# 2304 places for a sender block in place of 2560: a fifth slot tile of 64 lanes

## The chip, the cores and the metric

The kernel runs on one core of one Trainium2 chip. What counts is the device time of one launch, in microseconds (us). The core has TensorE (PE in the profile, with its weight loads as PEld), VectorE (DVE), ScalarE (ACT), GpSimd (POOL) and SyncE (SP, which here only issues DMAs).

## The reference

Four graph networks run one after the other on the same graph of 3125 nodes with 128 features and 53125 directed edges; each adds to `x`, and a layer norm follows. Cut to what matters:

```python
# L0: gated network, 2 rounds; edge_type has 8 values
trans = einsum('nh,tdh->tnd', h, edge_W[l]);  msgs = trans[edge_type, src]
agg = segment_sum(msgs, dst);                 h = relu(gru(agg, h))
# L1: three relational layers
msg = xw[etype, src] / count(etype, dst);     agg = segment_sum(msg, dst)
h = res + relu(agg + x @ root + bias)
# L2: normed sum over receivers, gathered at the sender
msgs = norm * x[col];                         agg = segment_sum(msgs, row)
# L3: means of edge_attr over dst and over src, and a two-layer network
```

The edges are sorted by `dst`; `src` is in no order. All is float32.

## The kernel before

A **sender block** is 126 nodes; there are `TB = 25`. Each edge has a place in its sender's block, in the order of the edges. A block has `CAP` places, and four places side by side are one lane's record: a row of 4 x 128 numbers in the DRAM tensor `chunks`. 128 such rows, so 512 places, are a **slot tile**; `QS = 5` tiles a block make 2560 places, and `NQ = 125` tiles in all. The fullest block of this input has 2226 edges. Tiles are numbered by turn first: tile `n` is turn `n // 25` of block `n % 25`, so tiles 100 to 124 are the fifth turn of the 25 blocks.

The program has these stages, which follow one another in the trace.

- **First loop** (about 100 to 604 us): 52 groups of 1024 edges. GpSimd gathers message rows (L694), PE sums them by receiver (L834), counts marks (L842, whose result is 56 lanes high) and puts each edge's payload into its place (L848). VectorE then unpacks the places (`slots`).
- **First layer's tiles** (676 to 834 us): for each of 125 tiles VectorE makes a one-hot (L1901), PE spreads the block's rows over the lanes in four products (`spread_slots`, L956), ScalarE copies the result from PSUM to `xs` (L1301, 6 buffers), and SP stores it to `chunks` (L561).
- **First layer's sums** (837 to 1070 us): for each of 149 windows of 21 receivers GpSimd gathers 128 rows of `chunks` (L694), VectorE makes one-hots, and PE sums in four products (`sum_window`, L984). Every 12 windows follows a `transform` (L969).
- **Layers 2 to 4** (1172 to 2238 us): tiles and window sums are interleaved by a written order (`plan`, `joined`). In a layer's tail, two tiles stand for three windows. In layers 3 and 4 GpSimd also scatters attributes (L703) between its gathers.
- **Targets** (2290 to 2490 us): rows are spread and scattered to `chunks` (L1174, L792).
- **Block sums** (2494 to 2637 us): for each block, its five slot tiles are loaded back (L679, with the attributes, L680) and summed in 4 products of 144 columns each (L1198); after the next block's third tile the block is turned by two small products (L1186 and L1187; L1187's result is 16 lanes high).

A float32 product is in the trace as two records, each with its own weight load. A record of 128 x 128 is called a pair below. In the built programs each matmul carries the part of the array that it uses: it is the whole one (128 rows by 128 columns) for nearly all, 128 rows by 64 columns for L842, 128 by 32 for L1187 and 32 by 128 for L1147.

If a block had more edges than places, flags would send the program to a slow general path (`general`); this input does not take it before or after.

Of the kernel before, what the change touches and what calls it, by code (L numbers as in the profile page):

```python
# [16 lines left out]
ALU = mybir.AluOpType  # L17
ACT = mybir.ActivationFunctionType
# [3 lines left out]
P = 128  # L22
# [4 lines left out]
TB = 25  # L27
NV = TB * P
BS = 126
# [6 lines left out]
A = 16  # L36
# [12 lines left out]
SPAN = 512  # L49
QS = 5  # L50
NQ = TB * QS
# [1 line left out]
QCOLS = 4 * TB  # L53
NEAR = 3 * QCOLS
NEAR_STEPS = (24, 40)
CAP = QS * SPAN
WD = 21
WT = WD * T
NW = -(-NODES // WD)
# [6 lines left out]
NGRP = -(-NW // GW)  # L66
RECORD_COLS = 4 * P + 4
FAR_CODE = 32767
RECS = NQ * P
RS, DS, SS, XS, NS = 6, 4, 4, 6, 3  # L70
RANKS = TB * CAP
YW = 5
# [74 lines left out]
def graph_kernel(nc, xT_d, dst_rows_d, dst_d, src_d, typ_d, mark_d, w_d, b_d, iota_d, out_d):  # L147
    with ExitStack() as ctx:
# [291 lines left out]
        def plan(k):  # L440
# [9 lines left out]
                at.append((NQ + v if k == 1 else when, 1, "sums", v))  # L450
            return [(kind, n) for _, _, kind, n in sorted(at)]

        def tile_no(k, i):

            return JOINED[i] if k >= 3 else i
# [60 lines left out]
        def _(eng):  # L516
# [32 lines left out]
            def layer(k):  # L549
                if k == 2:  # L550
                    eng.wait_ge(q("lanes_ready"), 2)
                    eng.dma_start(targets_d.rearrange("(a r) p -> r a p", a=5), trow_u8[0:NWP * 4 // 5])\
                       .then_inc(q("lanes_stored"), 16)
                def store_tile(k, i):
                    n = tile_no(k, i)
                    after(eng, "x1_evac", k, i + 1)
                    if k == 1:
                        eng.wait_ge(q("code_put"), i + 1)
                    cols = RECORD_COLS if k == 1 else 4 * P
                    at = (n % TB * QS + n // TB) * P  # L560
                    eng.dma_start(x1_d[at:at + P, 0:cols], xs[:, i % XS, 0:cols])\  # L561
                       .then_inc(q(f"x1_stored_{i % XS}"), 16)
                    ahead = n // QS + NS - 1
                    if k >= 3 and n in (20, 25, 30):
                        for s in {20: (), 25: (6,), 30: (7, 8)}[n]:
                            lanes_load(k, s)
                    elif n % QS == 0 and ahead < TB:
                        lanes_load(k, ahead)
                    if k == 2 and i in (10, 18):
                        inv_load((i - 10) // 8)  # L570
                    if k >= 3 and n in (27, 36):
                        after(eng, "agg_evac", k - 1, NTRI)
                        inv_load((n - 27) // 9)
                    if k == 3 and n == 42:
                        attrs_sent(eng, 2)
                        attr_load(attrs_1, AT[3])
                    if k == 3 and n == 60:
                        attr_load(attrs_0, AT[5])
                    if k == 4 and n == 42:
                        attrs_sent(eng, 3)  # L580
                        attr_load(attrs_1, AT[4])
                    if 2 <= k < 4 and n == NQ - 1:
                        for s in range(NS - 1):
                            lanes_load(k + 1, s)

                if k == 1:
                    for i in range(NQ):
                        store_tile(1, i)
                    eng.wait_ge(q("inv_ready"), INV_PIECES)
                    eng.dma_start(inv_d, acc[TYPE_ROWS, 0:NU]).then_inc(q("inv_stored"), 16)  # L590
                    after(eng, "acc_evac", 1, NGRP)
                    general(1)
                    attrs_sent(eng, 1)
                    attr_load(attrs_0, AT[2][:6])
                    eng.wait_ge(q("attr_loaded"), 48)
                    after(eng, "gru_h", 1, NCH)
                    attr_load(attrs_1, AT[2][6:])
                    for s in range(NS - 1):
                        lanes_load(2, s)
                    return  # L600
                for kind, j, i in joined():
                    if kind == "tile":
                        store_tile(j, i)
                    if kind == "sums" and i >= GW and i % GW == 5 and i // GW + 1 < NGRP:
                        after(eng, "agg_evac", j, 4 * (i // GW))
                        inv_load(i // GW + 1)
                after(eng, "acc_evac", 4, NGRP)
                for j in (2, 3, 4):
                    general(j)
# [66 lines left out]
            for i in range(NQ):  # L676
                if i >= GR:
                    eng.wait_ge(q("gcn_sum"), i - GR + 1)
                eng.dma_start(grec[:, i % GR, 0:4 * P], x1_d[i * P:(i + 1) * P, 0:4 * P]).then_inc(q(f"x1_stored_{i % GR}"), 16)  # L679
                eng.dma_start(grec[:, i % GR, 4 * P:], attr_d[i * 4 * P:(i + 1) * 4 * P, :].rearrange("(p j) a -> p (j a)", j=4))\  # L680
                   .then_inc(q(f"x1_stored_{i % GR}"), 16)
            eng.wait_ge(q("gcn_added"), NCH)
            eng.wait_ge(q("turn_used"), NCH)
# [114 lines left out]
        def _(eng):  # L798
# [143 lines left out]
            def spread_slots(k, i):  # L942
# [9 lines left out]
                elif k >= 3:  # L952
                    after(eng, "x1_evac", k - 1, NQ)
                after(eng, "shot", k, i + 1)
                for j in range(4):
                    last = mm(ps[:, STAGE1_BANKS[i % 3], j * P:(j + 1) * P], shot[0:BS, i % SS, j * P:(j + 1) * P],  # L956
                              hrow[0:BS, sb_, :], start=True, stop=True)
                last.then_inc(q("stage1_mm"), 1)

# [230 lines left out]
            for i in range(NQ):  # L1190
                b, first_tile, last_tile = i // QS, i % QS == 0, i % QS == QS - 1
                if first_tile and b >= 2:
                    eng.wait_ge(q("sums_kept"), b - 1)
                eng.wait_ge(q("ghot"), i + 1)
                record_got(eng, i)
                for j in range(4):
                    got = grec[:, i % GR, :].rearrange("p (m s a) -> p s m a", s=4, a=A)[:, j]
                    last = mm(ps[0:BS, 6 + b % 2, 0:P + A], ghot[:, i % GH, j, :], got, start=first_tile and j == 0,  # L1198
                              stop=last_tile and j == 3)
                last.then_inc(q("gcn_sum"), 1)  # L1200
                if i % QS == 2 and b >= 1:
                    turn(b - 1)
# [39 lines left out]
        def _(eng):  # L1242
# [51 lines left out]
            def layer(k):  # L1294
                def keep_tile(k, i):
# [2 lines left out]
                        slot_wait(eng, "x1_stored", XS, k, NQ, i - XS)  # L1298
                    elif k >= 3:
                        slot_wait(eng, "x1_stored", XS, k - 1, NQ, range(i, NQ, XS)[-1])  # L1300
                    act(xs[:, i % XS, 0:4 * P], ps[:, STAGE1_BANKS[i % 3], :], ACT.Copy).then_inc(q("x1_evac"), 1)  # L1301

                def keep_sums(k, gi):
                    after(eng, "xf_mm", k, gi + 1)
# [125 lines left out]
        def _(eng):  # L1430
# [304 lines left out]
            def slots():  # L1735

                eng.wait_ge(q("placed"), NG + 1)
                st.do(vec.tensor_copy(pay_i, ps[:, 7, 0:NTILE]))
                st.did(vec.tensor_scalar(src1_i, pay_i, 15, None, ALU.arith_shift_right))
                st.did(vec.tensor_scalar(code_i, pay_i, 32767, None, ALU.bitwise_and))  # L1740
                st.settle()
# [36 lines left out]
            def place_cells():  # L1778
                eng.wait_ge(q("starts_mm"), 1)
                st.did(vec.tensor_copy(starts, ps[0:TB, 7, 0:NWP]))  # L1780
                st.did(vec.tensor_scalar(col640, lane_no[0:TB], float(QS * P), None, ALU.mult))
                st.settle()
                st.did(vec.tensor_tensor(origin, chunk0, starts, ALU.subtract))
                st.did(vec.tensor_tensor(ends, starts, cells, ALU.add))
# [448 lines left out]
```

## Time and profile before

| | |
|---|---|
| median of 3 runs | 2705.34 us (2699.7 to 2707.08) |
| profiled execution, its own time | 2699.8 us |
| its span | 2697.7 us |
| PE busy | 2415.3 us, 90% of the span |
| PEld, DVE, POOL, ACT busy | 80%, 68%, 59%, 32% |
| mean granted clock of TensorE | 0.969 |
| DMA moved | 520.18 MB, 193 GB/s on the mean |

The profiled execution is one run; its rows are read against its own 2699.8 us, of which 2.1 us lie outside the span. The busy share is a mean over stages with different limits, so the stages have to be read one by one.

### The profile page before, as it was taken

The numbers are of one execution on the slowest core, as the hardware profiler recorded it, in microseconds if no ns is written. First come the engines' busy times: TensorE is split into PE (matmuls) and PEld (weight loads), VectorE is DVE, ScalarE is ACT, GpSimd is POOL, SyncE is SP. The second block draws the span as 40 slices with busy tenths as digits, with TensorE's granted clock in tenths as the row PEclk, the third lists the DMA queues.
The fourth block names the chain that finished last, engine by engine and source line by source line (L and its number), as shares of the span: only waits on it lengthen the run. The fifth ranks groups of instructions, "written<-read, shape, count | busy, mean of one in ns | idle before, by whom it ended". The sixth has DMA issues, their size and how long they took to land.

```text
span 2697.7 us, 46297 instructions
## 1 busy us (share of the span) xinstructions
PE 2415.3 (90%) x15920; PEld 2163.0 (80%) x15920; DVE 1847.5 (68%) x6137; ACT 857.8 (32%) x1498; POOL 1596.6 (59%) x1706
## 2 busy tenths in 40 slices
PE   7698888887878999889999999999899988886998
PEld 3587777773777998569999989999899976876996
DVE  4887777766775876687676589675578864443884
ACT  3476665652442111332222322122222201443002
POOL 0777777765556665755666367775477772776000
PEclk9899999998989999999999999999999997998999
DMA  8422222212887664188998789887998861776990
GB/s 297 124 64 63 61 63 64 62 50 91 257 249 212 176 179 138 32 241 285 277 283 261 238 283 282 265 263 235 288 275 272 261 196 31 238 258 233 269 264 31
DMA packets 271663, 520.18 MB, mean 193 GB/s; under 512 B 62015, under 2 KB 115698, under 8 KB 270645
## 3 DMA queue, kind: packets, MB, share of 16 engines
q1 hardware_dynamic: 185197, 289.49, 34.8%
q0 software_dynamic: 86224, 227.59, 29.0%
q8 instruction: 136, 2.23, 0.3%
q14 instruction: 106, 0.87, 0.1%
HBM read 323.93 MB, written 192.99 MB: 192 GB/s over the span
## 4 chain that ended last, share of the span: by engine, by line
PE 49%; POOL 20%; DMA 14%; issue 8%; DVE 7%; ACT 2%; SPq 0%; DVEq 0%; POOLq 0%; ACTq 0%
PE ps L984 18%; POOL msg L694 11%; PE ps L956 8%; PE ps L969 5%; PE ps L1198 5%; DMA rec<-chunks,idx 4%; POOL rec L694 4%; DMA chunks<-xs 3%; DMA chunks<-xo,put_idx 3%; POOL attributes L703 2%; PE ps L848 2%; POOL chunks L792 2%; DVE shot L1901 1%; PE ps L1174 1%; PE ps L1018 1%
## 5 line engine op out<-in xcount | busy, mean ns | idle before, releaser
L694 POOL DMA_INDIRECT rec<-chunks,idx x596 | 592.9, 995 | 368.1 <-PE ps L984 140.1
L984 PE MATMUL ps<-dhot,rec 128*128 128x168 f32 x4768 | 738.8, 310 | 50.9 <-DMA rec<-chunks,idx 37.7
L984 PEld LDWEIGHTS ps<-dhot,rec 128*128 128x128 f32 x4768 | 693.4, 191 | 70.7 <-issue 38.5
L1922 DVE TENSOR_SCALAR dhot<-iota,dcode 128x168 f32<-128x168 f32 x2384 | 593.2, 313 | 89.9 <-PE ps L984 80.3
L956 PE MATMUL ps<-hrow,shot 126*128 126x128 f32 x4000 | 504.4, 281 | 47.5 <-DVE shot L1901 33.7
L956 PEld LDWEIGHTS ps<-hrow,shot 126*128 126x128 f32 x4000 | 484.2, 196 | 59.2 <-issue 29.5
L694 POOL DMA_INDIRECT msg<-messages,idx_buf x416 | 401.6, 965 | 196.1 <-issue 195.5
L1301 ACT ACTIVATE xs<-ps 128x512 f32<-128x512 f32 x500 | 297.4, 597 | 672.2 <-PE ps L956 618.9
L703 POOL DMA_INDIRECT attributes<-w,rank_to x368 | 372.8, 1013 | 178.4 <-issue 120.6
L1901 DVE TENSOR_SCALAR shot<-srow,lane_no 126x512 f32<-126x512 uint8 x500 | 231.8, 489 | 93.2 <-DMA srow<-lanes_of_slots 46.8
L848 PE MATMUL ps<-big,lane1h 128*128 128x300 f32 x832 | 224.0, 422 | 1.8 <-ACT big L1284 1.8
L1964 DVE TENSOR_TENSOR agg_rows<-ps,tmp 128x504 f32<-128x504 f32 (+1 forms) x150 | 101.6, 677 | 158.6 <-PE ps L984 157.3
L848 PEld LDWEIGHTS ps<-big,lane1h 128*128 128x128 f32 x832 | 153.8, 190 | 56.7 <-issue 9.1
L792 POOL DMA_INDIRECT chunks<-xo,put_idx x149 | 148.1, 994 | 79.7 <-ACT xo L1408 50.4
L1279 ACT ACTIVATE tmp<-iota,slot_col 128x300 f32<-128x300 f32 x416 | 186.2, 530 | 10.4 <-DVE slot_col L1573 10.3
L969 PE MATMUL ps<-agg_rows,w 128*128 128x252 f32 (+1 forms) x832 | 178.6, 368 | 0.0
L1174 PE MATMUL ps<-yrows,thot 126*128 126x128 f32 (+1 forms) x1192 | 151.0, 285 | 28.7 <-ACT xo L1408 28.5
L1174 PEld LDWEIGHTS ps<-yrows,thot 126*128 126x128 f32 (+1 forms) x1192 | 142.4, 197 | 36.6 <-ACT xo L1408 35.9
L969 PEld LDWEIGHTS ps<-agg_rows,w 128*128 128x128 f32 x832 | 151.3, 190 | 15.2
L834 PE MATMUL ps<-onehot,msg 128*128 128x128 f32 x832 | 105.9, 281 | 53.5 <-DMA msg<-messages,idx_buf 53.5
L2117 DVE TENSOR_SCALAR thot<-trow,lane_no 126x512 f32<-126x512 uint8 x149 | 77.8, 524 | 107.9 <-PE ps L1174 107.3
L834 PEld LDWEIGHTS ps<-onehot,msg 128*128 128x128 f32 x832 | 99.2, 194 | 64.8 <-issue 64.8
(289 smaller groups left out, 2545.0 us busy)
## 6 DMA issues: line engine op xcount, KB each, us to landing
chunks<-xs SPq DMA_DIRECT2D x375, 256.0 KB, 4.7
tmp<-inverse_counts SPq DMA_DIRECT2D x36, 1008.0 KB, 10.1
chunks<-xs SPq DMA_DIRECT2D x125, 258.0 KB, 5.7
srow<-lanes_of_slots SPq DMA_DIRECT2D x100, 320.0 KB, 5.3
grec<-chunks SPq DMA_DIRECT2D x125, 256.0 KB, 3.0
messages<-big SPq DMA_DIRECT2D x25, 504.0 KB
trow<-lanes_of_targets SPq DMA_DIRECT2D x30, 320.0 KB, 4.0
rec<-chunks,idx POOLq DMA_INDIRECT x596
```

The lines of the kernel that those rows point to most:

```text
L694: eng.indirect_dma_start(buf, None, table, bass.IndirectOffsetOnAxis(ap=index, axis=0)).then_inc(sem, 16)
L703: eng.indirect_dma_start(attr_d, bass.IndirectOffsetOnAxis(ap=rank_to[:, c:c + 1], axis=0), attr_rows(k, n // G)[:, n % G * TC + T:(n % G ...
L792: eng.indirect_dma_start(x1_d, bass.IndirectOffsetOnAxis(ap=put_idx[:, v:v + 1], axis=0), xo[:, v % XO, :], None)\
L834: last = mm(ps[:, g % 2, 0:P], msg[:, g % SUB, t, :], onehot[:, g % 2, t, :], start=t == 0, stop=t == G - 1)
L848: last = mm(ps[:, 7, near_col(g):near_col(g) + NEAR], lane1h[:, g % 2, t, :], big[:, g % 2, t * NEAR:(t + 1) * NEAR], start=False, stop=Fa ...
L956: last = mm(ps[:, STAGE1_BANKS[i % 3], j * P:(j + 1) * P], shot[0:BS, i % SS, j * P:(j + 1) * P], hrow[0:BS, sb_, :], start=True, stop=True)
L969: last = mm(out, wt(REL[k], T)[:, t * P:(t + 1) * P], agg[gi % 2][:, t, 0:c1 - c0], start=t == 0, stop=k == 1 and t == T - 1)
L984: last = mm(ps[:, 4 + i % 2, (v % 3) * WT:(v % 3 + 1) * WT], rec[:, v % RS, j * P:(j + 1) * P], dhot[:, v % DS, j * WT:(j + 1) * WT], star ...
L1174: last = mm(ps[:, STAGE1_BANKS[v % 3], j * P:(j + 1) * P], thot[0:nodes_of(c), v % SS, j * P:(j + 1) * P], yrows[0:nodes_of(c), c, :], sta ...
L1301: act(xs[:, i % XS, 0:4 * P], ps[:, STAGE1_BANKS[i % 3], :], ACT.Copy).then_inc(q("x1_evac"), 1)
L1901: vec.tensor_scalar(shot[0:BS, i % SS, :], srow[0:BS, s_ % NS, (n % QS) * SPAN:(n % QS + 1) * SPAN], lane_no1[0:BS], None, ALU.is_equal).t ...
L1922: last = vec.tensor_scalar(dhot[:, v % DS, j * WT:(j + 1) * WT], iota[:, 0:WT], dcode[:, v, j:j + 1], None, ALU.is_equal)
```

## The change

The fifth tile of a block has 64 lanes in place of 128. A block has then 4 x 576 = 2304 places. In DRAM a block's rows are 576 apart, not 640. The fifth tile's products, PSUM copies, stores and loads cover 64 lanes; VectorE's one-hots stay 512 wide. The attributes have 57600 rows that are cleared before use, not 64000. VectorE clears the payload of the places that are no more, so that an overfull block is still found. The number of tiles, products, copies, stores, loads, gathers and scatters stays as it is.

```diff
-CAP = QS * SPAN
+LAST = P // 2
+ROWS = (QS - 1) * P + LAST
+CAP = 4 * ROWS
...
-RECS = NQ * P
+RECS = TB * ROWS
...
+        def lanes_in(turn):
+            return LAST if turn == QS - 1 else P
+
+        def rows_at(sb_, turn):
+            return sb_ * ROWS + turn * P
...
-                    at = (n % TB * QS + n // TB) * P
-                    eng.dma_start(x1_d[at:at + P, 0:cols], xs[:, i % XS, 0:cols])\
+                    at, lanes = rows_at(n % TB, n // TB), lanes_in(n // TB)
+                    eng.dma_start(x1_d[at:at + lanes, 0:cols], xs[0:lanes, i % XS, 0:cols])\
                        .then_inc(q(f"x1_stored_{i % XS}"), 16)
...
-                eng.dma_start(grec[:, i % GR, 0:4 * P], x1_d[i * P:(i + 1) * P, 0:4 * P]).then_inc(q(f"x1_stored_{i % GR}"), 16)
-                eng.dma_start(grec[:, i % GR, 4 * P:], attr_d[i * 4 * P:(i + 1) * 4 * P, :].rearrange("(p j) a -> p (j a)", j=4))\
+                at, n = rows_at(i // QS, i % QS), lanes_in(i % QS)
+                eng.dma_start(grec[0:n, i % GR, 0:4 * P], x1_d[at:at + n, 0:4 * P]).then_inc(q(f"x1_stored_{i % GR}"), 16)
+                eng.dma_start(grec[0:n, i % GR, 4 * P:], attr_d[4 * at:4 * (at + n), :].rearrange("(p j) a -> p (j a)", j=4))\
...
+                n = lanes_in(tile_no(k, i) // TB)
                 for j in range(4):
-                    last = mm(ps[:, STAGE1_BANKS[i % 3], j * P:(j + 1) * P], shot[0:BS, i % SS, j * P:(j + 1) * P],
+                    last = mm(ps[0:n, STAGE1_BANKS[i % 3], j * P:(j + 1) * P], shot[0:BS, i % SS, j * P:j * P + n],
                               hrow[0:BS, sb_, :], start=True, stop=True)
...
+                n = lanes_in(i % QS)
                 for j in range(4):
-                    got = grec[:, i % GR, :].rearrange("p (m s a) -> p s m a", s=4, a=A)[:, j]
-                    last = mm(ps[0:BS, 6 + b % 2, 0:P + A], ghot[:, i % GH, j, :], got, start=first_tile and j == 0,
+                    got = grec[0:n, i % GR, :].rearrange("p (m s a) -> p s m a", s=4, a=A)[:, j]
+                    last = mm(ps[0:BS, 6 + b % 2, 0:P + A], ghot[0:n, i % GH, j, :], got, start=first_tile and j == 0,
...
-                    act(xs[:, i % XS, 0:4 * P], ps[:, STAGE1_BANKS[i % 3], :], ACT.Copy).then_inc(q("x1_evac"), 1)
+                    n = lanes_in(tile_no(k, i) // TB)
+                    act(xs[0:n, i % XS, 0:4 * P], ps[0:n, STAGE1_BANKS[i % 3], :], ACT.Copy).then_inc(q("x1_evac"), 1)
...
                 st.do(vec.tensor_copy(pay_i, ps[:, 7, 0:NTILE]))
+                st.do(vec.memset(pay_i[LAST:, (QS - 1) * QCOLS:], 0))
...
-                st.did(vec.tensor_scalar(col640, lane_no[0:TB], float(QS * P), None, ALU.mult))
+                st.did(vec.tensor_scalar(col640, lane_no[0:TB], float(ROWS), None, ALU.mult))
```

No instruction changes its place on PE, but the half tiles lie in two kinds of surroundings, which the program's order shows. A row gives the line, the operation, what is written from what, the result's partitions x columns, and how many follow one another. On PE, at the end of the first layer's tiles (L956 spreads them, L984 starts the window sums), there stands before:

```order
L926 MATMUL ps<-h,w 128x126
L956 MATMUL ps<-hrow,shot 128x128 x220
L949 MATMUL ps<-flags,w 128x6
L956 MATMUL ps<-hrow,shot 128x128 x280
L984 MATMUL ps<-dhot,rec 128x168 x68
L969 MATMUL ps<-agg_rows,w 128x252 x8
```

and with the change, where the last 100 products (25 tiles of 4) are 64 lanes high and stand together:

```order
L935 MATMUL ps<-h,w 128x126
L966 MATMUL ps<-hrow,shot 128x128 x220
L958 MATMUL ps<-flags,w 128x6
L966 MATMUL ps<-hrow,shot 128x128 x180
L966 MATMUL ps<-hrow,shot 64x128 x100
L994 MATMUL ps<-dhot,rec 128x168 x68
L979 MATMUL ps<-agg_rows,w 128x252 x8
```

The one row of 280 products has become one of 180 and one of 100. In the second layer's tail PE has before, with two tiles (x8) between three window sums (x12):

```order
L956 MATMUL ps<-hrow,shot 128x128 x8
L984 MATMUL ps<-dhot,rec 128x168 x12
L956 MATMUL ps<-hrow,shot 128x128 x8
L984 MATMUL ps<-dhot,rec 128x168 x8
L969 MATMUL ps<-agg_rows,w 128x252 x8
L972 MATMUL ps<-x,w 128x252
L984 MATMUL ps<-dhot,rec 128x168 x4
L956 MATMUL ps<-hrow,shot 128x128 x8
L984 MATMUL ps<-dhot,rec 128x168 x12
```

and with the change:

```order
L966 MATMUL ps<-hrow,shot 128x128 x8
L994 MATMUL ps<-dhot,rec 128x168 x12
L966 MATMUL ps<-hrow,shot 64x128 x8
L994 MATMUL ps<-dhot,rec 128x168 x8
L979 MATMUL ps<-agg_rows,w 128x252 x8
L982 MATMUL ps<-x,w 128x252
L994 MATMUL ps<-dhot,rec 128x168 x4
L966 MATMUL ps<-hrow,shot 64x128 x8
L994 MATMUL ps<-dhot,rec 128x168 x12
```

The tiles' rows are now half high: from tile 100 on the 25 half tiles of such a layer stand in 13 places, each between full products. In the built program L956 uses 128 rows by 64 columns of the array there, and the fifth tile's products in the block sums use 64 rows by 128 columns (25 places, one a block, between the fourth tile and the next block's first).

## Rows read from the trace of the kernel before

**Rows 1.** Windows by stage, core 0: span, its us, busy us (count) by engine, clock, DMA.

```profile
core 0: us, PE busy (x) PEld busy (x) DVE busy (x) ACT busy (x) POOL busy (x), PEclk, DMA share, GB/s
680.00:835.00 155.00, 124.17 (x973) 118.62 (x971) 105.20 (x189) 71.86 (x123) 93.08 (x180) 0.94 0.91 264
1180.00:1540.00 360.00, 350.01 (x2557) 342.49 (x2557) 249.79 (x810) 90.24 (x155) 200.63 (x197) 0.99 0.89 270
1540.00:1890.00 350.00, 334.49 (x2410) 327.11 (x2409) 256.38 (x811) 79.44 (x136) 238.56 (x237) 0.99 0.87 266
1890.00:2230.00 340.00, 314.31 (x2209) 303.21 (x2209) 246.25 (x791) 67.44 (x117) 237.25 (x237) 0.98 0.85 258
2490.00:2630.00 140.00, 135.73 (x1050) 128.24 (x1051) 110.96 (x526) 2.91 (x5) 0.00 (x0) 0.97 0.92 263
```

**Rows 2.** Waits in 790:835, the end of the first layer's tiles.

```profile
ACT xs L1301 <- DMA chunks<-xs: 16.7, 19, 3.1
POOL xs L751 <- DMA chunks<-xs: 15.2, 12, 2.6
```

**Rows 3.** Timeline of SP's queue, 675:836: start, us, queue, line, issue.

```profile
798.34 6.11 SPq L561 DMA_DIRECT2D chunks<-xs  x5
...
816.79 17.23 SPq L561 DMA_DIRECT2D chunks<-xs  x14
```

**Rows 4.** Timeline of PE in the second layer's tail, 1395:1410.

```profile
1402.40 1.95 PE L956 MATMUL ps<-hrow,shot 126*128 126x128 f32 x16
1404.19 3.59 PE L984 MATMUL ps<-dhot,rec 128*128 128x168 f32 x24
1407.61 1.95 PE L956 MATMUL ps<-hrow,shot 126*128 126x128 f32 x16
```

**Rows 5.** Timeline of PE in the first loop: one group's products.

```profile
265.39 2.02 PE L834 MATMUL ps<-onehot,msg 128*128 128x128 f32 x16 [1.27 <-DMA msg<-messages,idx_buf]
267.34 1.96 PE L842 MATMUL ps<-onehot,marks 128*56 128x128 f32 x16
269.23 4.31 PE L848 MATMUL ps<-big,lane1h 128*128 128x300 f32 x16
273.37 0.50 PE L817 MATMUL ps<-sb1h,w 128*128 128x200 f32 x2
```

**Rows 6.** Groups of weight loads, shapes apart: busy us, mean ns, idle before.

```profile
L956 PEld LDWEIGHTS ps<-hrow,shot 126*128 126x128 f32 x4000 | 484.2, 196 | 59.2 <-issue 29.5 <-ACT xs L1301 24.4 <-ACT hrow L1291 1.8
...
L842 PEld LDWEIGHTS ps<-onehot,marks 128*56 128x56 f32 x832 | 88.9, 130 | 6.4 <-issue 0.2
```

**Rows 7.** Timeline of PE in the block sums near the end.

```profile
2583.12 5.17 PE L1198 MATMUL ps<-grec,ghot 128*126 128x144 f32 x40
2588.13 0.39 PE L1186 MATMUL ps<-w,sums 126*128 126x126 f32 x2
2588.44 0.39 PE L1187 MATMUL ps<-w,sums 126*16 126x126 f32 x2
2588.76 5.17 PE L1198 MATMUL ps<-grec,ghot 128*126 128x144 f32 x40
```

**Rows 8.** Waits in 1750:1822, the third layer's tail.

```profile
POOL rec L694 <- issue: 8.2, 27, 0.3
...
PE ps L984 <- DMA rec<-chunks,idx: 2.2, 3, 1.2
```

**Rows 9.** Waits in 2182:2240, the fourth layer's end.

```profile
PE ps L984 <- DMA rec<-chunks,idx: 8.5, 9, 2.4
...
POOL rec L694 <- issue: 4.9, 16, 0.3
```

**Rows 10.** The page's part 5: gathers of messages in the first loop.

```profile
L694 POOL DMA_INDIRECT msg<-messages,idx_buf x416 | 401.6, 965 | 196.1 <-issue 195.5
```

**Rows 11.** Windows over 50 products of 8 rows by 1 column (L1147).

```profile
2312.00:2315.00 3.00, 3.00 (x29) 3.00 (x28) 0.49 (x1) 0.60 (x1) 2.39 (x3) 1.00 0.83 331
2318.00:2321.00 3.00, 3.00 (x14) 2.99 (x15) 0.15 (x1) 0.15 (x1) 0.96 (x1) 0.50 0.48 176
```

## Prediction

> **What bounds the kernel now.** I read the stages first, in the windows: PE is busy for 350 of 360 us in the second layer, 334 of 350 in the third, 314 of 340 in the fourth and 136 of 140 in the block sums, so there PE's own instructions count one for one unless something else shows [rows 1]. The first layer's tiles are different: PE has 124 us of work in 155, while the DMA engines are 91% busy at 264 GB/s [rows 1]. The waits of its last 45 us say what is short: ScalarE waits 16.7 us and GpSimd 15.2 us for stores of `xs` to free a buffer [rows 2]. In the first loop the page shows 416 gathers with 195.5 us of "issue" before them and nothing else: GpSimd never waits for data there [rows 10], so work of others that gets shorter in that loop gives nothing.
>
> **Stores of the first layer.** The last 25 tiles are the half ones, and they stand together, with nothing between them. SP's queue stores tiles 96 to 100 until 804.45 and tiles 111 to 124 until 834.02 [rows 3], so the 24 tiles after tile 100 take 29.6 us, 1.23 us each. What is left if stores cost half: PE's 8 pairs a tile at 112 ns (16 pairs from 1402.40 to 1404.19 [rows 4]) are 0.90 us, or 21.5 us for 24 tiles. The DMA engines have then 24 x 0.13 MB, three loads of lanes of 0.33 MB and up to six full stores of 0.26 MB that are in flight at 804: 5.7 MB, 22 us at 264 GB/s. Both limits lie at 22 to 22.5 us. **Term 1: -7 us.** Bounds: -9 (the DMA backlog is gone at once and nothing replaces it) and -3 (half of the gain goes to GpSimd, which copies codes and scatters attributes between the tiles, and to landing times that don't shrink with the size).
>
> **Stores of layers 2 to 4.** The tail tiles store half there too. But in the second layer's tail PE runs from one group to the next without a gap [rows 4]; in the third PE waits 2.2 us for gathers, and GpSimd, which issues them, has only waits of 0.3 us before 27 of them [rows 8]. It issues as fast as it can, so the gathers come late because of their number and not of the DMA engines' load. I take nothing for these stores. If the load did matter, all waits for gathers in the two tails would be the bound, 2.2 + 8.5 us [rows 8, 9].
>
> **What a half-high product costs.** The trace has a stand-in: L842 runs 16 pairs of 128 columns with a result 56 lanes high, on 128 rows by 64 columns of the array, between full products. From the first L834 to the first L848 32 pairs take 269.23 - 265.39 = 3.84 us [rows 5]; full pairs at 112 ns would take 3.58 [rows 4]. So one visit to the half array costs 0.26 us more, although its weight load is shorter (130 ns against 196 [rows 6]): the shorter load gives nothing visible, and going in and out costs. L1187 says the same for another partition: L1186 and L1187, four pairs of 126 columns, take 2588.76 - 2588.13 = 0.63 us [rows 7] where 0.45 would do, and the 40 pairs behind them 5.01 [rows 7] where 4.97 is the price between the 112 ns of 128 columns and the 142.5 of 168 (24 pairs in 3.42 us [rows 4]): 0.2 us together. I take 0.25 us a visit; the start of L834 behind a wait may be 0.1 of it, and I keep 0.15 and 0.3 as its ends.
>
> The Trainium skill has this rule in "TensorEngine Tiling (Array Packing)", section "Key Properties": changing the tiling mode, and not just the tile, drains the TensorE. By that rule, the trace agrees. The same skill's "TensorE: Matmul & The Clock Gate", section "LDWEIGHTS (loading the stationary operand)", gives a load's time as its columns over 1.2 GHz, so a load of 64 columns would save 53 ns; were the load the limit of each pair, the 100 + 300 products of two pairs would save 42 us and the sum below would be -38. The trace disagrees on the pair, as the row on L842 shows [rows 5].
>
> **Visits in layers 2 to 4.** With two tiles between three window sums, the 25 half tiles stand in 13 places a layer. Second layer: PE has no gap there, so 13 x 0.25 = **+3.3 us** (2 to 4). Third: the same 3.3, less the 2.2 us in which PE waits for gathers in that tail anyway [rows 8]: **+1.1 us** (0 to 3). Fourth: the gathers set the end, PE waits 8.5 us for them behind its last tile [rows 9], and they go out at GpSimd's own pace: **0** (0 to 2; if that cover were gone, 3.3). First layer: one visit, inside term 1. What is queued behind a late product is the window sum that frees a gather buffer; with six buffers GpSimd is not held up by 0.25 us.
>
> **Block sums.** The fifth tile has 64 rows in the contraction: 64 rows by 128 columns of the array, once a block, 25 visits between full products. No row of before shows just this kind; the nearest by cost are the two above, and for its sort L1147 (8 rows), whose pairs run at full clock at 103 ns (29 in 3.00 us [rows 11]), so a partial contraction doesn't slow a pair. PE has no gap in a block of 5.64 us [rows 7], and its products don't get shorter, since they have 144 columns as before. The loads become 10% smaller, but PE doesn't wait for them. 25 x 0.25 = **+6.3 us**. Bounds: 0 (this kind switches free) and 10 (0.4 a visit).
>
> **The rest.** The clearing of the attributes is 10% shorter, and the marks behind it in SP's queue arrive earlier; the first group starts earlier, but the loop ends when GpSimd's gathers end [rows 10]: 0. One small clearing on VectorE and its semaphore after the loop: +0.2. Copies by ScalarE and one-hots by VectorE keep their width along a lane: 0.
>
> **The sum.** -7 + 3.3 + 1.1 + 0 + 6.3 + 0.2 = +3.9 us. Against the profiled execution's own 2699.8 us that is 2703.7; that execution lies 5.5 us below the median of the runs, to which I add: 2705.3 + 3.9 = **2709 us**. About 0.3%, 8 us, is what a measurement of this kernel can tell from no change.
>
> **Rivals.**
> 1. *The half array at its first position is entered and left for free*, or the price hides in the gaps: terms 2 to 4 are then 0 to 3, the sum -5 to -7, 2699 us. For it: L842 and L1187 both write other partitions than 0, the new products start at 0. Against: what must be waited for is the full products' end, wherever the partition is. 15%.
> 2. *Faster, by the DMA engines.* They are 85 to 92% busy in the layers and block sums [rows 1]. If gathers come earlier once 25 stores a layer are half, PE's waits in the tails of layers 3 and 4 go: -10.7 [rows 8, 9], with term 1 at -9, against visits of 9.8 (3.3, 6.3, 0.2): -10, 2695 us. It decides for "faster" from 0.45 us of earlier landing a window on. Against: GpSimd's steady 0.3 us before each gather. 10%.
> 3. *Faster, by the short weight load.* If L956's pairs were held by the load alone and not, as L842 tells, by the 128 columns, 66 ns (196 - 130 [rows 6]) come off 600 pairs of layers 2 to 4: -40 us at most, 2670. Against: L842's 16 pairs start to start are 118 ns apart with the exit in them [rows 5], more than L956's 112. 3%.
> 4. *Slower: each switch shows a whole weight load.* If the load behind a switch can't be done beside the last products, each visit has 196 ns [rows 6] twice, 0.4 to 0.5 us, and the block sums 12, the second layer 6, the third 4: sum +15, 2720 us. For it: nobody measures the 64-row kind here. It decides from 0.42 us a visit on. 17%.
> 5. *Slower: the clock.* 50 small products of L1147 end at half clock (1.00 before, 0.50 after, with 14 pairs in 3 us for 29 [rows 11]). If 25 half tiles in a row do the same, their pairs take some 214 ns, 43 us for 25 tiles where 30 stand now: +13 in place of -7, 2729 us. Against: L842's products have 128 columns like these and the loop keeps its clock. 6%.
>
> **How the numbers follow.** Forecast 49%, its own range 2702 to 2716 (terms at their inner bounds: -9 + 2 + 0 + 3.8 + 0.2 below, -4 + 4 + 3 + 7.5 + 0.2 above). Faster by over 0.3%: rivals 2 and 3, with a sixth of rival 1: 13%. Slower: rivals 4 and 5 and a fifth of the forecast, whose upper end is past +8: 32%. Within: 55%. The range of 8 in 10 goes from 2698 (rival 1 in it, rivals 2 and 3 out) to 2721 (most of rival 4 in, rival 5 out).
>
> **What the new profile would show.** Right: the stores of tiles 101 to 124 pass in about 22 us; the distance from a tile pair's first product to the window sum's grows from 1.79 us by 0.1 and more, with PEld idle before the window's load; a block takes 5.85 to 5.95 us and not 5.64; the first loop's end stays. Wrong: block at 5.64 (rival 1), waits for gathers under 4 us in the fourth layer's end (rival 2), 16 half pairs in 1.3 us (rival 3), a block of 6.1 (rival 4), a granted clock under 1 in the first layer's last 25 us (rival 5). What would upset the whole most is term 1: if another buffer than `xs` paces the half tiles, up to 4 us of the gain are missing.

## The result, and the profile after

| | before | after |
|---|---|---|
| median, runs on the same chip | 2701.38 us (2693.21 to 2707.08, 5 runs) | 2721.38 us (2706.14 to 2725.5, 5 runs) |
| ratio after to before | | 1.0057, interval 1.0034 to 1.0080 |
| profiled execution, its own time and span | 2699.8 and 2697.7 us | 2725.5 and 2723.3 us |
| PE, PEld busy | 2415.3, 2163.0 us | 2447.7, 2179.0 us |
| mean granted clock | 0.969 | 0.959 |
| DMA moved | 520.18 MB | 502.95 MB |

The change makes the kernel 0.57% slower, 15 us of 2701 (9 to 22). The forecast was 3.9 us slower, so "within 0.3%" was the likeliest of its cases, and "slower" at 32% is what came. The time lies at the very end of the range of 2698 to 2721: 1.0057 of the 2705.3 us that the forecast starts from is 2720.8, and the median itself is 0.4 past it.

In the end of the first layer's tiles the stores now pass faster. SP's queue in 795:836 (start, us, queue, line, issue), where the first row is tiles 96 to 100; behind it stand five, five and 14 stores (before: [rows 3]):

```profile
797.77 5.08 SPq L569 DMA_DIRECT2D chunks<-xs  x5
...
803.57 4.68 SPq L569 DMA_DIRECT2D chunks<-xs  x5
...
812.98 11.61 SPq L569 DMA_DIRECT2D chunks<-xs  x14
```

From 802.85 to 824.59 tiles 101 to 124 take 21.7 us, where [rows 3] gave 29.6. The waits of 790:835 say the same (engine, tile and line, what is waited for: us in total, times, longest):

```profile
POOL xs L760 <- DMA chunks<-xs: 8.2, 8, 1.8
ACT xs L1313 <- DMA chunks<-xs: 8.2, 12, 1.8
```

They were 15.2 and 16.7 us in [rows 2]. Stores that free `xs` still hold ScalarE up, half as long.

The second layer's tail, timeline of PE after in 1399:1410, to be read beside [rows 4]:

```profile
1400.80 3.69 PE L994 MATMUL ps<-dhot,rec 128*128 128x168 f32 x24
1404.42 1.96 PE L966 MATMUL ps<-hrow,shot 126*64 126x128 f32 x16
1406.31 3.69 PE L994 MATMUL ps<-dhot,rec 128*128 128x168 f32 x24
1409.92 1.96 PE L966 MATMUL ps<-hrow,shot 126*64 126x128 f32 x16
```

From one tile pair to the next it is 1409.92 - 1404.42 = 5.50 us, where [rows 4] gives 5.21. The pair's 16 products to the window's first take 1.89 us (1.79 before), the 24 products of the sums 3.61 (3.42 before). So a third of the price falls between a pair's first product and the sums' first, and two thirds between that and the next pair. The weight loads of the same stretch have a gap at each change of shape, where before has none:

```profile
1404.41 1.72 PEld L966 LDWEIGHTS ps<-hrow,shot 126*64 126x64 f32 x16 [0.18 <-issue]
1406.31 3.43 PEld L994 LDWEIGHTS ps<-dhot,rec 128*128 128x128 f32 x24 [0.17 <-issue]
```

```profile
2583.26 5.55 PE L1209 MATMUL ps<-grec,ghot 128*126 128x144 f32 x40
2588.65 0.39 PE L1196 MATMUL ps<-w,sums 126*128 126x126 f32 x2
2588.96 0.39 PE L1197 MATMUL ps<-w,sums 126*16 126x126 f32 x2
2589.28 5.55 PE L1209 MATMUL ps<-grec,ghot 128*126 128x144 f32 x40
```

A block takes 2589.28 - 2583.26 = 6.02 us and not 5.64. All of it is in the 40 products (2588.65 - 2583.26 = 5.39 us, 5.01 before), eight of which are the fifth tile's.

The groups of weight loads with shapes apart (busy us, mean ns, idle before) show what the smaller loads are worth:

```profile
L966 PEld LDWEIGHTS ps<-hrow,shot 126*128 126x128 f32 x3200 | 386.7, 196 | 53.9 <-issue 28.2 <-ACT xs L1313 20.5 <-ACT hrow L1302 1.8
...
L966 PEld LDWEIGHTS ps<-hrow,shot 126*64 126x64 f32 x800 | 86.2, 137 | 8.8 <-issue 7.5 <-ACT xs L1313 1.2
...
L1209 PEld LDWEIGHTS ps<-grec,ghot 64*126 64x126 f32 x200 | 25.6, 184 | 3.7
```

A load of 64 columns is 59 ns shorter, yet 16 pairs take as long as before and more. The load of 64 rows by 126 columns is hardly shorter than one of 128 rows by 126, which takes 190 ns before.

The waits for gathers in the tails of layers 3 (1750:1822) and 4 (2182:2240) after:

```profile
PE ps L994 <- DMA rec<-chunks,idx: 0.6, 2, 0.4
...
PE ps L994 <- DMA rec<-chunks,idx: 10.1, 7, 3.0
```

In the third the cover of 2.2 us [rows 8] has been used up; in the fourth the 8.5 us [rows 9] are still there.

Last, this execution has something that the change doesn't explain. Windows over the last products before the end (stretch, its us, busy us and count by engine, clock, DMA):

```profile
2655.00:2676.00 21.00, 21.00 (x64) 14.91 (x64) 4.39 (x7) 3.82 (x7) 0.00 (x0) 0.50 0.00 1
```

The granted clock is half here, 1.2 GHz, and not 2.4. It fell in the stretch just before, behind the block sums, in which PE was busy for about half of the time:

```profile
2653.00:2656.00 3.00, 1.55 (x5) 0.76 (x5) 0.35 (x1) 0.27 (x1) 0.00 (x0) 0.70 0.02 5
```

Whether that belongs to the change is a question for a second execution of the same kernel, below.

### The profile page after: what moved, and what is told of

Read it like the earlier page. It is cut to its first block, busy times and chain, and to the rows that moved or that the text cites. A ratio compares the mean times of both kernels' runs of the same rounds, so it can differ in the third digit from the quotient of the medians.

```text
span 2723.3 us, 46298 instructions
## 1 busy us (share of the span) xinstructions
PE 2447.7 (90%) x15920; PEld 2179.0 (80%) x15920; DVE 1847.0 (68%) x6138; ACT 857.1 (31%) x1498; POOL 1592.6 (58%) x1706
## 2 busy tenths in 40 slices
DMA packets 262063, 502.95 MB, mean 185 GB/s; under 512 B 60415, under 2 KB 114098, under 8 KB 261045
## 4 chain that ended last, share of the span: by engine, by line
PE 53%; POOL 20%; DMA 11%; issue 8%; DVE 6%; ACT 2%; SPq 0%; DVEq 0%; POOLq 0%; ACTq 0%
PE ps L994 21%; POOL msg L703 15%; PE ps L966 10%; PE ps L979 6%; PE ps L1209 5%; DMA rec<-chunks,idx 3%; DMA chunks<-xo,put_idx 3%; POOL rec L703 2%; DMA chunks<-xs 2%; POOL chunks L801 2%; POOL attributes L712 1%; PE ps L1028 1%; PE ps L1184 1%; DVE shot L1914 1%; PE ps L1034 1%
## 5 line engine op out<-in xcount | busy, mean ns | idle before, releaser
L966 PE MATMUL ps<-hrow,shot 126*128 126x128 f32 (+1 forms) x4000 | 499.5, 280 | 45.3 <-DVE shot L1914 37.9
L966 PEld LDWEIGHTS ps<-hrow,shot 126*128 126x128 f32 (+1 forms) x4000 | 472.9, 184 | 62.8 <-issue 35.7
L1313 ACT ACTIVATE xs<-ps 128x512 f32<-128x512 f32 (+1 forms) x500 | 296.2, 596 | 669.7 <-PE ps L966 629.2
L979 PEld LDWEIGHTS ps<-agg_rows,w 128*128 128x128 f32 x832 | 151.3, 190 | 15.2
```

The source lines that it names most:

```text
L966: last = mm(ps[0:n, STAGE1_BANKS[i % 3], j * P:(j + 1) * P], shot[0:BS, i % SS, j * P:j * P + n], hrow[0:BS, sb_, :], start=True, stop=True)
L979: last = mm(out, wt(REL[k], T)[:, t * P:(t + 1) * P], agg[gi % 2][:, t, 0:c1 - c0], start=t == 0, stop=k == 1 and t == T - 1)
L1313: act(xs[0:n, i % XS, 0:4 * P], ps[0:n, STAGE1_BANKS[i % 3], :], ACT.Copy).then_inc(q("x1_evac"), 1)
```

## The experiments

**Half stores and copies, but all products full.** The fifth tile's products cover 128 lanes again, the DRAM layout, copies and stores stay as in the change; the loads too, but for block 0's fifth tile, which is loaded whole. If the products are the loss, this is the change's gain alone.

```diff
-                at, n = rows_at(i // QS, i % QS), lanes_in(i % QS)
+                at, n = rows_at(i // QS, i % QS), P if i == QS - 1 else lanes_in(i % QS)
...
-                n = lanes_in(tile_no(k, i) // TB)
...
-                    last = mm(ps[0:n, STAGE1_BANKS[i % 3], j * P:(j + 1) * P], shot[0:BS, i % SS, j * P:j * P + n],
+                    last = mm(ps[:, STAGE1_BANKS[i % 3], j * P:(j + 1) * P], shot[0:BS, i % SS, j * P:(j + 1) * P],
...
-                n = lanes_in(i % QS)
+                n = P
```

> The changed kernel with the products of the fifth tiles full again (128 lanes high in the layers, 128 rows in the block sums), while layout, stores, copies and loads stay half (only block 0's fifth tile is loaded whole, so that the lanes above 64 hold numbers). My theory: all of the loss is on PE, at the change between full and half products. Then the second layer's two-tile group goes back to 5.21 us per period, a block to 5.64 us, the first layer's tile stage still ends 8 us earlier than before, and the span is 2 to 8 us under the kernel before: ratio 0.997 to 0.999. Rival: the 576-row layout or the shorter DMAs cost something themselves; then the ratio stays over 1.000 with the PE periods back to normal.

Measured: ratio 0.9998 to before (0.9983 to 1.0013), median 2702.73 us of 12 runs. The layers' pairs and the blocks of the profile are those of before (1399.84 to 1405.04 is 5.20 us, a block 5.64):

```profile
1399.84 1.95 PE L965 MATMUL ps<-hrow,shot 126*128 126x128 f32 x16
1401.62 3.59 PE L993 MATMUL ps<-dhot,rec 128*128 128x168 f32 x24
1405.04 1.95 PE L965 MATMUL ps<-hrow,shot 126*128 126x128 f32 x16
```

So without the half products nothing is lost, and nothing that can be told from zero is won either; the ratio lies above the expected 0.997 to 0.999. The interval, -4.6 to +3.5 us, leaves out the -7 of term 1.

**Only the layers' products full.** The edit of L966 above alone; the block sums keep 64 rows.

```diff
-                n = lanes_in(tile_no(k, i) // TB)
...
-                    last = mm(ps[0:n, STAGE1_BANKS[i % 3], j * P:(j + 1) * P], shot[0:BS, i % SS, j * P:j * P + n],
+                    last = mm(ps[:, STAGE1_BANKS[i % 3], j * P:(j + 1) * P], shot[0:BS, i % SS, j * P:(j + 1) * P],
```

> Only the layers' products (L956 of before) are full again; the block sums keep their 64-row products. Theory of the visits: the second layer's period is 5.21 us, a block stays at 6.03 us, 25 x 0.39 = 9.8 us remain, less 3 to 8 us from the first layer: ratio 1.001 to 1.003. Rival, the clock: if the fall of the granted clock after the block sums (0.50 for 21 us, some 10 us of time) comes from the half-row products, it is seen here too and the ratio is 1.004 to 1.007.

Measured: 1.0037 (1.0015 to 1.0060), 2715.1 us of 6 runs. Against the kernel with all products full that is 0.39%, 10.5 us for the 25 visits of the block sums, 0.42 each. The profile gives 0.38: a block takes 6.02 us here. The ratio is above the theory's 1.001 to 1.003, and near what the rival on the clock gave; but the rival's sign is missing: no long half clock stands behind the block sums of this profile, where the stretch to the last network takes 16.2 us (16.1 before).

```profile
2582.97 5.55 PE L1208 MATMUL ps<-grec,ghot 128*126 128x144 f32 x40
2588.36 0.39 PE L1195 MATMUL ps<-w,sums 126*128 126x126 f32 x2
2588.68 0.39 PE L1196 MATMUL ps<-w,sums 126*16 126x126 f32 x2
2588.99 5.56 PE L1208 MATMUL ps<-grec,ghot 128*126 128x144 f32 x40
```

**Only the block sums full.**

```diff
-                at, n = rows_at(i // QS, i % QS), lanes_in(i % QS)
+                at, n = rows_at(i // QS, i % QS), P if i == QS - 1 else lanes_in(i % QS)
...
-                n = lanes_in(i % QS)
+                n = P
```

> Only the block sums' products are full again; the layers keep their half-high ones. Theory of the visits: period 5.51 us in the second layer's tail, a block 5.64 us; 3.9 us lost in the second layer, up to 2 in the third and fourth, 3 to 8 gained in the first: ratio 0.998 to 1.001. If the clock's fall after the block sums comes from the 64-row products it isn't seen here; if it is seen here too, it is chance or comes from elsewhere.

Measured: 1.0017 (1.0001 to 1.0034), 2707.94 us of 10 runs, a little over the expected 0.998 to 1.001: 0.19% or 5.1 us over all full, for the layers' products. The three add up: -0.5 (all full) + 10.5 (block sums) + 5.1 (layers) = 15.1 us, and the change as a whole measured 15. That they meet so closely is luck, since each has an interval of 4 us and more to either side.

**One product of four half.** Of each fifth tile only the fourth product stays half in the layers and in the block sums; the count of half products falls to a quarter, while the count of entries and exits stays in the block sums and doubles where two tiles stand together. (Block 0's fifth tile is loaded whole.)

```diff
-                n = lanes_in(tile_no(k, i) // TB)
...
+                    n = lanes_in(tile_no(k, i) // TB) if j == 3 else P
...
-                n = lanes_in(i % QS)
...
+                    n = lanes_in(i % QS) if j == 3 else P
```

> Of the four products of each fifth tile only the last is half (64 lanes high, 64 rows), three are full. Theory of the switch: the price hangs on going in and out, not on the number of half products, so a block stays at 6.03 us (5.64 + 0.39), and a two-tile group of the second layer, which now goes in and out twice, takes 5.21 + 0.60 = 5.8 us per period. Rival, slower pairs: each half product costs its share, so a block takes 5.64 + 0.10 = 5.74 us and the period 5.21 + 0.08 = 5.3 us.

Measured: one execution, 2728.51 us, which by itself says little. PE in the block sums:

```profile
2584.99 5.55 PE L1209 MATMUL ps<-grec,ghot 128*126 128x144 f32 x40
2590.39 0.39 PE L1196 MATMUL ps<-w,sums 126*128 126x126 f32 x2
```

```profile
1398.38 2.42 PE L966 MATMUL ps<-hrow,shot 126*128 126x128 f32 x16
1400.74 3.69 PE L994 MATMUL ps<-dhot,rec 128*128 128x168 f32 x24
1404.26 2.42 PE L966 MATMUL ps<-hrow,shot 126*128 126x128 f32 x16
1406.61 3.69 PE L994 MATMUL ps<-dhot,rec 128*128 128x168 f32 x24
```

From 1400.74 to 1406.61 it is 5.87 us, 0.66 over the 5.21 of [rows 4], where the change has 0.29: the price goes by visits and not by products. It is the price of a switch.

**Before, with half products and copies in the layers only.** The layout, stores and block sums are those of before; the upper 64 lanes of the fifth tile are stored with what `xs` held, which no edge of this input reads.

```diff
+                n = P // 2 if tile_no(k, i) // TB == QS - 1 else P
...
-                    last = mm(ps[:, STAGE1_BANKS[i % 3], j * P:(j + 1) * P], shot[0:BS, i % SS, j * P:(j + 1) * P],
+                    last = mm(ps[0:n, STAGE1_BANKS[i % 3], j * P:(j + 1) * P], shot[0:BS, i % SS, j * P:j * P + n],
...
-                    act(xs[:, i % XS, 0:4 * P], ps[:, STAGE1_BANKS[i % 3], :], ACT.Copy).then_inc(q("x1_evac"), 1)
+                    n = P // 2 if tile_no(k, i) // TB == QS - 1 else P
+                    act(xs[0:n, i % XS, 0:4 * P], ps[0:n, STAGE1_BANKS[i % 3], :], ACT.Copy).then_inc(q("x1_evac"), 1)
```

> The kernel before, with nothing changed but the height of the fifth turn's products and PSUM copies in the layers (64 lanes); layout, stores and loads are whole, and the block sums are as before. Theory of the visits: no gain in the first layer's tiles (they end as before, at 833 us), and the second layer's tail pays 13 x 0.30 = 3.9 us, the third and fourth up to 2 each: ratio 1.001 to 1.003. Rival: if the first layer's gain came from the products and not from the stores, the tiles end at 825 here too.

Measured: 1.0006 (0.9989 to 1.0023), 2701.04 us of 10 runs, against 2699.84 of 29. By time alone it can't be told from no change, nor from the expected 1.001 to 1.003, and the 1.6 us are less than the 5.1 that the kernel with only its block sums full gave for the same products. The profile has the switches (1405.47 - 1399.96 = 5.51 us) and a second layer of 329.6 us where kernels with full products have 323.6 to 326.3:

```profile
1399.96 1.96 PE L957 MATMUL ps<-hrow,shot 126*64 126x128 f32 x16
1401.85 3.69 PE L985 MATMUL ps<-dhot,rec 128*128 128x168 f32 x24
1405.47 1.96 PE L957 MATMUL ps<-hrow,shot 126*64 126x128 f32 x16
```

It also shows that term 1's base was not firm. Tiles 101 to 124, with whole stores, end 26.2 us after tile 100 here, not 29.6, and the last one ends at 826.56 us and not at the expected 833:

```profile
794.79 5.56 SPq L561 DMA_DIRECT2D chunks<-xs  x5
...
812.26 14.30 SPq L561 DMA_DIRECT2D chunks<-xs  x14
```

**Two more executions of before and one of after**, unchanged kernels, to see what an execution varies by in that stretch and in the last one.

> The kernel before once more, for a second profile. In its first profile the stretch between the first layer's sums and the second layer's first product took 77 us at a granted clock of 0.93, in all five kernels with the new layout 78.5 to 82 us at 0.83 to 0.87. If that is chance of the execution, this run has 78 to 82 us too; if it comes from the earlier end of the first layer's tiles or from the layout, it has 77 us at 0.93 again.

> The kernel before a third time, for one thing: how long its stores of tiles 101 to 124 take. 29.6 us in the profile that the prediction was made from, 24.6 to 26.2 in three other executions with whole stores, 21.7 to 23.2 in five of six with half stores. If the first profile was the odd one, this gives 24 to 26 us, and the half stores are worth 2 to 4 us and not 7.

> The changed kernel once more. Stores of tiles 101 to 124 in 21.5 to 23.5 us; block 6.03 us. In its first profile the clock stood at 0.50 for some 20 us behind the block sums, and the stretch from the first layer norm product to the first product of the last network took 27.0 us where all other kernels have 16.1 to 16.2. If the half-row products bring that, it is here again (the two other kernels with them did not show it); if it is chance, this run has 16 us and is some 10 us shorter than the first profile.

Measured: 2695.09, 2694.76 and 2709.91 us. In the second execution of before SP's queue has

```profile
796.85 5.90 SPq L561 DMA_DIRECT2D chunks<-xs  x5
...
814.80 12.68 SPq L561 DMA_DIRECT2D chunks<-xs  x14
```

which is 827.48 - 802.75 = 24.7 us for the 24 tiles; the third gives 26.6. Their last stores end at 827.5 and 829.2 us, with full products and full stores, so the 826.56 of the kernel with half products in its layers is no gain of theirs: it is the 834.0 of the first profile that stands alone. In the second execution of after the granted clock is 0.92 on the mean of the same stretch, so the 21 us at half clock were that one execution's:

```profile
2655.00:2676.00 21.00, 20.28 (x97) 14.38 (x97) 9.80 (x16) 4.47 (x9) 0.00 (x0) 0.92 0.00 1
```

The longer stretch behind the first layer's sums is chance too: from the last transform's end to the second layer's first tile product the three executions of before take 84.5, 85.9 and 87.9 us at a granted clock of 0.94, 0.88 and 0.86, and the two of after 87.6 and 84.1 us at 0.86 and 0.94.

**Before, without its own small switch.** The switches have a forerunner in the kernel before: L1187's product is 16 lanes high, 128 rows by 32 columns of the array, once a block. Here it has 128 lanes; the extra rows of `sums` are zeros, so the result is the same.

```diff
-                sums = three("sums", [P, 2, P + A])
+                sums = three("sums", [P, 2, 2 * P])
...
-                mm(in_chunk(ps[SRC_ROWS, 3 + c % 2, :], c, b), sums[0:BS, b % 2, P:], wb("ident", BS, BS), start=True, stop=True)\
+                mm(in_chunk(ps[:, 3 + c % 2, :], c, b), sums[0:BS, b % 2, P:], wb("ident", BS, BS), start=True, stop=True)\
...
+            st.did(vec.memset(sums[:, :, P:], 0.0))
...
-                vec.tensor_scalar(sums[0:BS, b % 2, P:], ps[0:BS, 6 + b % 2, P:P + A], deg[0:BS, 3, b:b + 1], None, ALU.mult)\
+                vec.tensor_scalar(sums[0:BS, b % 2, P + MT:P + MT + A], ps[0:BS, 6 + b % 2, P:P + A], deg[0:BS, 3, b:b + 1], None, ALU.mult)\
```

> The kernel before with one part-array product less per block: the 16-lane product that turns the attributes' sums is made 128 lanes high by a wider `sums` buffer with zeros. No half-row product is in the block sums at all. Theory of the visits: L1187 already cost 0.2 to 0.3 us a block by going in and out, so a block goes from 5.64 to 5.35 to 5.45 us, 25 times: -5 to -7 us, ratio 0.9975 to 0.9985. Rival: what costs at L1186 and L1187 is the wait for the sums or the small size itself; then a block stays at 5.64 us.

Measured: 0.9972 (0.9955 to 0.9989), 2693.55 us of 12 runs, 7.6 us faster than before. A block takes 2591.80 - 2586.45 = 5.35 us where it took 5.64. The turn's two products take 0.45 us of it (0.63 before) and the 40 behind them 4.90 (5.01):

```profile
2586.45 0.38 PE L1186 MATMUL ps<-w,sums 126*128 126x126 f32 x2
2586.68 0.39 PE L1187 MATMUL ps<-w,sums 126*128 126x126 f32 x2
2586.90 5.07 PE L1198 MATMUL ps<-grec,ghot 128*126 128x144 f32 x40
2591.80 0.38 PE L1186 MATMUL ps<-w,sums 126*128 126x126 f32 x2
```

**The change's layout with full products and a full turn.** The first experiment's kernel with the edit just above.

```diff
-                mm(in_chunk(ps[SRC_ROWS, 3 + c % 2, :], c, b), sums[0:BS, b % 2, P:], wb("ident", BS, BS), start=True, stop=True)\
+                mm(in_chunk(ps[:, 3 + c % 2, :], c, b), sums[0:BS, b % 2, P:], wb("ident", BS, BS), start=True, stop=True)\
```

> Half stores and loads of the fifth tile, all products full (as in the first experiment), and the attributes' turn full as well. Theory: the two gains are apart, so the first layer's tiles end 7 to 8 us earlier and a block takes 5.35 to 5.45 us: ratio 0.996 to 0.999, the fastest of all. Rival: the first layer's gain is given back behind it, as in the first experiment, and only the 5 to 7 us of the blocks stay: ratio 0.998.

Measured: 0.9962 (0.9947 to 0.9977), 2690.31 us of 12 runs: the fastest of all, 10 us under before. It can't be told from the one above, whose interval overlaps, so the smaller layout may still be worth nothing. Most blocks take 5.35 us, as above, but single ones up to 6.64, with PE waiting 0.5 and 0.4 us for loads and 1.0 for a one-hot, so the block sums take 138.2 us where the kernel above takes 136.0.

## Why the prediction held in its range, at the edge, and missed in its case

Its steps, with what the runs gave:

| step | forecast | measured |
|---|---|---|
| term 1, first layer's stores | -7 (-9 to -3) | -3 to -4 by the stretch; stores, loads and the rest together -0.5 (-4.6 to +3.5) by time |
| second layer | +3.3 | +3.3 by stage |
| third layer | +1.1 | +0.8 by stage, within the spread |
| fourth layer | 0 | 0 by stage |
| block sums | +6.3 (0 to 10) | +9.5 by stage, +10.5 by time |
| the rest | +0.2 | not separated |
| sum | +3.9 | +15 (9 to 22) by time |

The stages are means over the profiles of either kind, without the kernel with one half product of four: the second layer, from its first window sum to the last row of its last transform, takes 325.2 us with full products (seven profiles) and 328.5 with half ones (four), and the two groups don't overlap; the third, from there to the same place of its own, 358.6 and 359.4, where single profiles go from 357.6 to 360.2; the fourth 348.9 and 348.8. The 25 blocks take 142.2 us where products and loads are whole (four profiles) and 151.7 where the products are half (four, one of four half among them).

**What failed first is term 1**, the step "SP's queue stores tiles 96 to 100 until 804.45 and tiles 111 to 124 until 834.02, so the 24 tiles after tile 100 take 29.6 us". What the changed kernel would do there was right: 21.7 us, where "about 22" was forecast. What was wrong is what to subtract it from. Five profiles with whole stores give 29.6, 24.7, 26.6 (the three of before), 26.2 and 24.6 us, mean 26.3; seven with half stores 21.7, 22.7, 22.4, 22.2, 21.9, 23.2 and 28.2, mean 23.2, or 22.4 without the last, which stands alone and whose cause is open. A stretch that DMA paces varies by 5 us between executions of the same kernel (29.6 against 24.7), and the prediction took its one profile, by chance the slowest there, as the kernel's own. The gain is 3 to 4 us by these stretches, near the weak end of its bounds, for a reason that it hadn't named. By where the last store ends it is smaller still: 829.1 us on the mean with whole stores and 827.2 with half ones (826.5 without the same odd one). By time even less is seen. The half loads gave nothing: with them and full products the block sums take 143.1 and 143.5 us, not under 142.2.

**Then the block sums.** The mechanism was right, in and out of a part of the array costs PE time in which nothing else can run, but the size was taken from other parts of the array: 0.25 us, from the rows on L842 and L1187. The 64 rows by 128 columns cost 0.38 to 0.39 by the block's period, so a block takes 6.02 us where 5.85 to 5.95 was forecast. The stand-in L1187 was itself read too low: 0.2 us with 4.97 as the price of 40 undisturbed pairs, where they take 4.90 and the stay 0.29. The text had said that no row of before showed this kind; the upper bound of 10, at 0.4 a visit, held but for 0.5 us by time. These 3.2 us and term 1's 3 to 4 take +3.9 to about +10.5.

**The layers' visits** were sized well: 0.29 to 0.30 against 0.25 a visit. The second layer gives the forecast's 3.3 us, where 13 visits at 0.30 would be 3.9. In the third the waits for gathers were used up, and the 0.8 us agree with the forecast but can't be told from zero; in the fourth the waits held, as forecast. By the Trainium skill's "TensorEngine Tiling (Array Packing)", section "Key Properties", a change of tiling mode drains the TensorE. The trace agrees as far as it goes: 0.29 to 0.30 us per visit in the layers, the weight load behind each change starting 0.17 to 0.18 us after the one before it ended, and the same price when three of four half products are made full. It shows what a switch costs, not what happens inside it.

**The rivals.** 1, free entry at the first position: false, both kinds start at lane 0 and cost 0.29 and 0.38. 2, earlier gathers: false in the fourth layer, where the waits are 10.1 us and not fewer; the third's shrink from 2.2 to 0.6 while the switches make PE later by as much. 3, the short load: false, 137 ns against 196 and no pair any faster. 4, a whole load at each switch, 0.4 to 0.5 us a visit: not as a rule, since the layers pay 0.29, but the block sums at 0.38 come close to its threshold of 0.42, and its time of 2720 is nearer than the forecast's. It had the number and not the layers. (The 0.42 holds if the block sums alone pay more; with every visit at the same price v, the sum is 51v - 9 and passes +8 from v = 0.33 on.) 5, the clock: false in the first layer, where the stretch passes in 21.7 us at a granted clock of 1.00. The share for "faster" was also added up wrongly: 10 + 3 and a sixth of 15 are 15.5% and not 13.

**What stays open.** The steps measured by stage give -3.5 + 3.3 + 0.8 + 9.5 = about 10 us; the timed runs give 15, with 9 as the lower end. The timed experiments do add up to 15, so the rest, if it is not chance, lies in what the stages don't resolve: stores and loads gave 3 us less by time than by stretch, and the products cost 2 us more (15.6 against 13.6). Most of it goes with the clock. Over the 126 runs whose mean granted clock is on record, a run of the same kernel with 0.001 less of it was about 1.3 us longer (an estimate: one straight line, with a level of its own for each kernel and each group of runs). The five runs of after have 0.9616 on the mean and 55 of before 0.9650, which is 4 to 5 us; at the same clock the line leaves about 11 us for the change (give or take 4), and 9.2 and 3.6 for the products of the block sums and of the layers, where the stages have 9.5 and 4.1. Whether the half products bring the lower clock stays open: after has 0.9616, the kernel with half block sums alone 0.9628, with half layers alone 0.9631 and with all products full 0.9643, but before with half products in its layers has 0.9669.

The profiled execution adds some 10 us by its half clock at the end (27.0 us from the products behind the block sums to the last network's second, 2654.8 to 2681.8, where before takes 16.1 and the second execution of after 17.5), which no other kernel shows: the two others with half block sums take 16.2 us there. Why 64 rows cost 0.09 us more than 64 columns was not separated either. Half stores in the first layer alone, in the layout of before, were not tried. Nor was a fifth tile of 96 lanes: that the price hangs on the part of the array, and not on any smaller height, rests on the products of 126 rows or lanes that stand beside full ones without a gap [rows 4].

## What to carry to other kernels

Making a product smaller in lanes didn't make it shorter here, and where it made it use another part of the array than its neighbours, each stay there cost 0.3 to 0.4 us: look for single odd-shaped products between full ones, and pad them, which gave 0.28% (0.11 to 0.45) in the kernel before. Where a term is the difference of two stretches that DMA paces, take the base from several profiles and not one; here the base alone was off by 3 us of 7. A price taken from a neighbouring shape deserves its own upper bound in the likeliest case, not only in the range.

## What was not expected of the hardware

- The price of a stay depends on the part: 128 rows by 32 columns 0.29 us (5.64 against 5.35 a block), 128 by 64 0.29 (5.50 against 5.21 a group), 64 by 128 0.38 (6.02 against 5.64 a block).
- It is paid in full for a single product: 0.66 us for the two stays of one half product each.
- A load of 64 columns takes 137 ns and one of 128 takes 196, while one of 126 columns takes 190 with 128 rows and 184 with 64: rows hardly count.
- With whole stores the end of the first layer's tiles takes 24.6 to 29.6 us for the 24 stores behind tile 100, and 24.7 to 29.6 in three executions of one kernel.
